# A transformer layer's expert stage, run one batch at a time, with its tokens gathered by 32-row float32 matmuls

## The reference, cut to what matters

```python
x = layernorm(h)                                   # 2 x 1024 x 128
grouped = x.reshape(B, S // 16, 16, D)             # 64 groups of 16 tokens in a batch
logits = einsum('bgtd,des->bgtes', grouped, controller) + tie     # 64 experts (es)
perm = (logits == max(logits, over the 16 tokens))                # one token for each expert and group
inner = relu(einsum('bgtesf,bgtes->bgesf', einsum('bgtd,desf->bgtesf', grouped, f1), perm))   # f = 32
inter2 = einsum('bgesf,esfd->bgesd', inner, f2)
h = h + einsum('bgesd,bgtes->bgtd', inter2, perm)
```

## Time and profile before

| what | value |
|---|---|
| median of 3 runs | 509.86 us (508.5 to 510.01) |
| the profiled execution, its own time | 509.83 us |
| its span, first to last instruction | 508.1 us |
| TensorE clock granted, mean | 0.992 of full |
| busy: PE, DVE, ACT, POOL | 485.5, 405.3, 369.7, 238.3 us |

### The profile page before, as it was taken

One profiled execution on the slowest core, in us unless ns is written; L12 is line 12 of the kernel. 1 busy time (PEld: TensorE's weight loads), 2 busy tenths in 40 slices (PEclk: granted clock), 3 DMA queues, 4 the chain that ended last, 5 costly groups with the idle time before them and its releaser, 6 DMA issues.

```text
span 508.1 us, 10652 instructions
## 1 busy us (share of the span) xinstructions
PE 485.5 (96%) x3584; PEld 396.5 (78%) x3584; DVE 405.3 (80%) x752; ACT 369.7 (73%) x696; POOL 238.3 (47%) x234
## 2 busy tenths in 40 slices
PE   2999999999999999999999999999999999998887
PEld 2955788888888888888888888888888888894564
DVE  5369999878887886788877887788778899988752
ACT  1258788887788778877888788878887887743555
POOL 1102585766356635653266536654664436443000
PEclk9999999999999999999999999999999999997999
DMA  6500029333933493361640783087308730000002
GB/s 238 200 1 0 2 53 213 79 84 78 196 67 83 83 196 65 94 124 43 141 110 10 167 167 84 11 180 153 83 10 182 151 84 0 1 2 1 1 18 68
DMA packets 29608, 44.73 MB, mean 88 GB/s; under 512 B 3328, under 2 KB 21248, under 8 KB 29312
## 3 DMA queue, kind: packets, MB, share of 16 engines
q1 hardware_dynamic: 28992, 44.21, 37.4%
q10 hardware_dynamic: 576, 0.00, 0.1%
HBM read 6.46 MB, written 1.05 MB: 15 GB/s over the span
## 4 chain that ended last, share of the span: by engine, by line
PE 89%; DVE 6%; ACT 2%; DMA 2%; issue 1%; SPq 0%; POOL 0%; DVEq 0%; ACTq 0%
PE ps L688 23%; PE ps L672 21%; PE ps L656 11%; PE ps L657 11%; PE ps L598 5%; PE ps L731 3%; PE ps L593 2%; PE ps L866 2%; PE ps L660 2%; DMA arena<-in_wqkv_rows 2%; PE ps L877 1%; PE ps L568 1%; PE ps L802 1%; DVE pt_lo L1292 1%; DVE neg_max L1304 1%; DVE v_all L1369 1%
## 5 line engine op out<-in xcount | busy, mean ns | idle before, releaser
L425 POOL TENSOR_SCALAR probs<-probs,inv_sum 128x1024 f32<-128x1024 f32 x128 | 144.7, 1131 | 183.3 <-DVE inv_sum L1298 180.6
L1304 DVE TENSOR_REDUCE neg_max<-ps 128x1 f32<-128x1024 f32 x128 | 156.7, 1224 | 63.8 <-PE ps L660 63.7
L980 ACT ACTIVATE pt_hi<-ps 128x512 fp32r<-128x512 f32 x256 | 139.1, 595 | 39.6 <-PE ps L672 39.6
L1292 DVE TENSOR_TENSOR pt_lo<-ps,pt_hi 128x512 fp32r<-128x512 f32 x256 | 162.5, 677 | 1.5 <-ACT pt_hi L980 1.5
L688 PE MATMUL ps<-pt_hi,v_slot 128*128 128x256 f32 x512 | 149.9, 326 | 0.0
L1000 ACT ACTIVATE probs<-ps,neg_max 128x1024 f32<-128x1024 f32 x128 | 142.5, 1113 | 1.5 <-DVE neg_max L1304 0.7
L672 PE MATMUL ps<-ident,probs 128*128 128x128 f32 x1024 | 133.8, 274 | 0.7 <-DVE v_all L1201 0.6
L688 PE MATMUL ps<-pt_lo,v_slot 128*128 128x256 f32 x512 | 127.4, 280 | 0.0
L672 PEld LDWEIGHTS ps<-ident,probs 128*128 128x128 f32 x1024 | 109.9, 140 | 1.3 <-DVE v_all L1201 0.7
L688 PEld LDWEIGHTS ps<-pt_hi,v_slot 128*128 128x128 f32 x512 | 96.5, 188 | 9.7 <-issue 9.7
L688 PEld LDWEIGHTS ps<-pt_lo,v_slot 128*128 128x128 f32 x512 | 97.0, 190 | 8.8 <-issue 8.8
(11 more groups left out here) (149 smaller groups left out, 434.5 us busy)
## 6 DMA issues: line engine op xcount, KB each, us to landing
q_st<-arena SPq DMA_DIRECT2D x28, 256.0 KB, 3.7
k_hi<-arena SPq DMA_DIRECT2D x28, 256.0 KB, 5.1
k_lo<-arena SPq DMA_DIRECT2D x28, 256.0 KB, 5.3
v_slot<-v_all SPq DMA_DIRECT2D x14, 512.0 KB, 3.9
arena<-arena SPq DMA_DIRECT2D x28, 256.0 KB, 5.7
f_sb<-in_f SPq DMA_DIRECT2D x2, 1024.0 KB, 10.6
x<-in_tok SPq DMA_DIRECT2D x2, 512.0 KB, 7.5
w_slot<-in_w_pairs SPq DMA_DIRECT2D x8, 128.0 KB, 2.0
```

The costliest lines, as they stand in the source:

```text
L425: pool.tensor_scalar(probs[:, t % 4, :], probs[:, t % 4, :], inv_sum[:, t % 4:t % 4 + 1], 1.0, ALU.mult, ALU.mult).then_inc(norm_done, 1)
L980: act.activation(dst, ps[:, transposes_bank(t, a, drain), :].rearrange("p (j c) -> p j c", c=P), ACT.Copy).then_inc(hi_done, 1)
L1292: dve.tensor_tensor(pt_lo[at], ps[:, transposes_bank(t, a, drain), :].rearrange("p (j c) -> p j c", c=P), pt_hi[at].bitcast(F32), ALU.subt ...
L1304: dve.tensor_reduce(neg_max[:, t % 4:t % 4 + 1], ps[:, SCORES + 2 * (t % 2):SCORES + 2 * (t % 2) + 2, :].rearrange("p a c -> p (a c)"), AX ...
```

## The change

What it does, engine by engine:

- Gathering without `quad`, `spread`, and the split into high and low parts. ScalarE (and for part of the second batch VectorE) copies the transposed choices plainly into `chosen`. Each pair of groups (32 tokens) is then gathered by one float32 matmul whose stationary operand is 32 rows of `x2` and whose moving operand is 32 rows of `chosen`, four pairs at a time on four row strips, each in its own bank (`take(b, r)`: four tiles, 16 float32 matmuls, four banks). The four results are copied, one bank at a time (`take_copy`).
- GpSimd loses `token_high` and `token_low` and two small setup instructions.
- The layer is done for one batch, then the other, with 64 groups as moving columns instead of 128: `first_product(b)` is 64 matmuls of 64 columns, in two halves of eight `k`; `second_product(b, half)` is 32 matmuls of 64 columns. Each is called twice as often as before. The first batch's gathering stands around the second's transposes; its two products around the second's choices.
- `hidden` is rectified by ScalarE in three of the four halves and by VectorE in the last.
- Rows: `row_transposes(n)` and `results(n)` handle two tiles at a time (8 transposes, 8 float32 matmuls); ScalarE copies the first bank and VectorE the second; VectorE adds 256 columns at once; SyncE stores 128 KB at a time, 8 times instead of 16.
- `LAST_OUTPUTS` is reordered: head 0 columns 0, head 1 columns 0, last values, head 0 columns 1, head 1 columns 1. VectorE makes the first batch's choices before it adds any of these, instead of after the third.

```diff
-        LAST_OUTPUTS = [(0, 0, WORK), (0, 1, TRANS), (1, 0, TRANS + 1), (1, 1, WORK)]
+        LAST_OUTPUTS = [(0, 0, WORK), (1, 0, TRANS), (0, 1, TRANS + 1), (1, 1, WORK)]
...
-                        if (k, t) == (1, 4) and pair.i == 7:
-                            pool.wait_ge(scores_ready, B * SPB - SPH)
-                            token_high(0)
-                        if (k, t) == (1, 5) and pair.i == 7:
-                            token_high(1)
...
             clear_choices(0)
-            token_low(0)
-            token_low(1)
             deviations(4)
             deviations(5)
             pool.wait_ge(logit_mm, 1)
             clear_choices(1)
-            token_low(2)
-            token_low(3)
```

TensorE's new helpers and its new list:

```diff
+            def take(b, r):
+
+                pe.wait_ge(chosen_done, 2 * b + 2)
+                if b == 1 and r == 0:
+                    pe.wait_ge(hid_left, 2)
+                for t in range(4 * r, 4 * r + 4):
+                    for j in range(PPT):
+                        if t == 4 and r == 1:
+                            take_copied(b, 0, j)
+                        rows = slice(32 * j, 32 * (j + 1))
+                        ins = pe.matmul(ps[:, TAKE_BANKS[b] + j, t % 4 * P:(t % 4 + 1) * P], x2[rows, NT * b + t, :],
+                                        chosen[rows, t, :], start=True, stop=True, tile_position=(32 * j, 0))
+                        if t % 4 == 3:
+                            ins.then_inc(taken_mm, 1)
+
+            def first_product(b):
+
+                for j in range(PPT):
+                    take_copied(b, 1, j)
+                for k in range(NK):
+                    for q in range(4):
+                        e = NK * q + k
+                        ins = pe.matmul(ps[32 * q:32 * (q + 1), HIDDEN_BANKS + k // 8, k % 8 * PAIRS:(k % 8 + 1) * PAIRS],
+                                        f1_sb[:, e * F:(e + 1) * F], taken[b][:, e, :], start=True, stop=True,
+                                        tile_position=(0, 32 * q))
...
+            def second_product(b, half):
...
+                for k in range(8 * half, 8 * half + 8):
+                    for q in range(4):
+                        rows = slice(F * q, F * (q + 1))
+                        ins = pe.matmul(ps[:, INTER_BANKS[b] + q, k % 8 * PAIRS:(k % 8 + 1) * PAIRS], f2_sb[rows, k, :],
+                                        hidden[b][rows, k, :], start=True, stop=True, tile_position=(F * q, 0))
...
             choice_transposes(0)
+            take(0, 0)
             for t in range(NT):
                 pe.wait_ge(x2_done, NT + t + 1)
                 ins = pe.transpose(ps[:, TRANS + t // 4, (t % 4) * P:(t % 4 + 1) * P], x2[:, NT + t, :], ident[:, :])
-            take(range(0, 1))
+            take(0, 1)
             pe.wait_ge(x2t_done, 4)
             expert_logits(1, PV_BANK).then_inc(logit_mm, 1)
-            take(range(1, 5))
+            first_product(0)
+            second_product(0, 0)
             choice_transposes(1)
...
+            take(1, 0)
+            second_product(0, 1)
+            take(1, 1)
+            row_transposes(0)
+            first_product(1)
+            results(0)
+            row_transposes(1)
+            second_product(1, 0)
+            results(1)
+            row_transposes(2)
+            second_product(1, 1)
+            results(2)
+            row_transposes(3)
+            for n in range(3, 8):
+                if n < 7:
+                    row_transposes(n + 1)
+                results(n)
```

ScalarE's new list, on which several steps rest:

```diff
+            choice_copy(0, 0)
+            choice_copy(0, 1)
+            for j in range(PPT):
+                take_copy(0, 0, j)
             for c in range(2):
                 act.wait_ge(x2t_mm, c + 1)
                 act.activation(x2t[:, (2 + c) * HALF:(3 + c) * HALF], ps[:, TRANS + c, :], ACT.Copy
                                ).then_inc(x2t_done, 1)
...
+            for j in range(PPT):
+                take_copy(0, 1, j)
+            rectify(0, 0)
+            rectify(0, 1)
+            inter_copies(0, 0)
+            choice_copy(1, 0)
+            take_copy(1, 0, 0)
+            take_copy(1, 0, 1)
+            inter_copies(0, 1)
+            take_copy(1, 1, 0)
+            take_copy(1, 1, 1)
+            row_copy(0)
+            rectify(1, 0)
+            row_copy(1)
+            inter_copies(1, 0)
+            row_copy(2)
+            inter_copies(1, 1)
+            for n in range(3, 8):
+                row_copy(n)
```

More of the change, by code:

```diff
@@ L541, in _ @@
             run_pairs(sp, pair_loads)
-            for t in range(TILES):
-                sp.wait_ge(result_done, t + 1)
-                sp.dma_start(out[t * P:(t + 1) * P, :], result[:, t, :]).then_inc(stored, 16)
-            sp.wait_ge(stored, 16 * TILES)
+            for n in range(TILES // 2):
+                sp.wait_ge(result_done, n + 1)
+                sp.dma_start(out[2 * n * P:2 * (n + 1) * P, :].rearrange("(t p) d -> p t d", p=P),
+                             result[:, 2 * n:2 * n + 2, :]).then_inc(stored, 16)
+            sp.wait_ge(stored, 16 * TILES // 2)
         @block.tensor
@@ new lines, in inter_copied, with row_transposes @@
+            def inter_copied(n):
+                pe.wait_ge(int_left, 2 * n + 2)
+                pe.wait_ge(int_right, 2 * n + 2)
+            def row_transposes(n):
+                b, g = ROWS[n]
+                if g == 0:
+                    inter_copied(2 * b + 1)
+                for side in range(2):
+                    for j in range(PPT):
+                        first = 2 * (NT * j + 2 * g + side)
+                        ins = pe.transpose(ps[:, ROW_BANKS[n] + side, j * P:(j + 1) * P],
+                                           inter_t[b][:, first:first + 2, :].rearrange("p u e -> p (u e)"), ident[:, :])
+                    ins.then_inc(intp_mm, 1)
@@ new lines, in results @@
+            def results(n):
+                b, g = ROWS[n]
+                pe.wait_ge(intp_left, n + 1)
+                pe.wait_ge(intp_right, n + 1)
+                if n >= 2:
+                    pe.wait_ge(result_done, n - 1)
+                for side in range(2):
+                    t = 2 * g + side
+                    for j in range(PPT):
+                        ins = pe.matmul(ps[32 * j:32 * (j + 1), RESULT_BANK + n % 2, side * D:(side + 1) * D],
+                                        perm[:, PPT * (NT * b + t) + j, :], inter_p[b][:, t, j, :],
+                                        start=True, stop=True, tile_position=(0, 32 * j))
+                ins.then_inc(res_mm, 1)
@@ L1018, in _ @@
             run_pairs(act, pair_steps)
-            def take(tiles):
-                for i in tiles:
-                    act.wait_ge(taken_mm, i + 1)
-                    act.activation(taken[:, :, 8 * i:8 * i + 8],
-                                   ps[:, TAKEN + i % 4, :].rearrange("p (g e) -> p e g", e=ES), ACT.Copy).then_inc(taken_done, 1)
             for t in range(PV_LAG):
@@ L1370, in _, with take_copy, inter_copies @@
-            for i in range(TILES):
-                dve.wait_ge(res_mm, i + 1)
-                dve.tensor_tensor(result[:, i, :], ps[:, i % 4, 0:D], h_sb[:, i, :], ALU.add).then_inc(result_done, 1)
+            def take_copy(r, j):
+                dve.wait_ge(taken_mm, PPT * (2 + r) + j + 1)
+                dve.tensor_copy(*take_parts(1, r, j)).then_inc(taken_right, 1)
+            def inter_copies(b, half):
+                dve.wait_ge(int_mm, 2 * b + half + 1)
+                for q in range(2, 4):
+                    dve.tensor_copy(*inter_parts(b, half, q)).then_inc(int_right, 1)
@@ L1375 @@
+            inter_copies(1, 0)
+            add_residual(1)
+            row_copy(2)
+            inter_copies(1, 1)
+            add_residual(2)
+            row_copy(3)
+            for n in range(3, 8):
+                if n < 7:
+                    row_copy(n + 1)
+                add_residual(n)
 SETUP_DIAG = 4
```

250 lines of the change are left out of this document (111 added, 139 removed).

## The result

The changed kernel takes 501.94 us (median of 4 runs, 501.19 to 502.61) where the kernel before, on the same chip, takes 509.18 (507.94 to 510.01): ratio 0.9861, 95% interval 0.984 to 0.9882. Measured again later it came to 501.79 (501.56 to 502.17). Predicted were 500.4, between 498.0 and 505.0. The profiled execution took 501.19 us, 499.4 of them the span.

A forecast was written before the change was run, and what follows sets the result against it. VectorE, then low-clocked TensorE, then copies, then TensorE's last loop were taken to set the pace. TensorE's 28.5 us list led to the last addition at 495.9; plus 0.6, 2.2 and 1.73 outside the span: 500.4 us, range 498.0 to 505.0.

The forecast's parts named there:

- Unit prices: Times per TensorE operation: 56 ns for a four-strip group of the 64-column first product, 109 for second product and gathering.
- The far bound of the second product: Second product with 64 columns: 56 ns for a group of four strips at best, where 109 was taken.
- the walk: Step-by-step timing of the new instruction lists from 452.71 us, putting the last addition's end at 495.93.
- The last loop: Row transposes and results at the end: 1.60 us for each pair of tiles, TensorE the bound, half the shape changes saved.
- the likeliest case: The forecast itself, 500.4 us, with no fall of TensorE's clock in the layer; chance 0.45.
- The rival of one fall: TensorE's clock falls again once, at half speed for 6.8 us, costing 1.8 us at the end: 502.2; chance 0.20.
- the slower side: Clock stays at 1.2 GHz from 462.6 us through the whole layer, end 23.2 us later, 523.6; chance 0.03.
- Waits: TensorE's waits before third gathering, first row transposes, first product 1 and last results: 1.2, 0.7, 0.4, 0.3, together 2.6 us.
- Tail: From the last addition to the span's end: 1.93 us as before plus 0.3 for the larger store, 2.2 us.
- the sum is 28.5 us: TensorE's own list from batch 0's first product at 466.74 us to 495.26: products, transposes, gatherings, results, shape changes and waits.
- fault of the walk: An unnamed error in the step-by-step timing that costs 1 to 8 us; chance 0.07.
- The rival in which the second product gains as well: Second product also gains from 64 columns: 2.8 us faster, about 497.6; chance 0.05.

The follow-up runs named there:

- e10: The changed kernel with two unused GpSimd subtractions put beside VectorE's comparisons of the second batch: 501.95 us, ratio 0.9846.
- e3: The kernel before with only its last loop changed to two tiles a turn, copies shared by ScalarE and VectorE: 506.48 us, ratio 0.9935.
- e4: The kernel before with only its gathering changed to 32-row float32 matmuls, the layer still in one piece: 513.46 us, ratio 1.0081.
- e2: The kernel before with six constant matmuls in TensorE's wait before the second batch's transposes: 508.11 us, ratio 0.9963.
- e7: The changed kernel with the first batch's second product run whole ahead of the second batch's gatherings: 502.21 us, ratio 0.9861.
- e8: The kernel before with the 32-row float32 gathering, plus 28 constant matmuls in TensorE's waits between gatherings: 510.4 us, ratio 1.0001.
- e9: The changed kernel with 72 one-column matmuls (144 instructions) in a wait ahead of the second batch's first gathering: 500.39 us, ratio 0.9819.
- e11: The changed kernel with VectorE making two copies of the first batch's second gathering, plus 60 tiny matmuls: 499.1 us, ratio 0.9792.
- e5: The changed kernel with VectorE making two of four copies of the first batch's second gathering, and choice copies moved earlier: 501.01 us, ratio 0.9832.
- e1: The changed kernel with 128 increments of an unused semaphore ahead of all TensorE work: 513.9 us, ratio 1.0082.

## Why the prediction was right, and where it was not

Right, and by its own mechanisms:
- *Unit prices.* From first product to second 1.92 us, less 0.14 for the change of shape, over 32 groups: 56 ns, as taken. By the rule of the Trainium skill (TensorE: Matmul & The Clock Gate, Part 3) that a weight load overlaps running matmuls only when its row group differs, it would have been 81 and, with the change of shape, 2.7 us, an estimate; the trace disagrees. The far bound of the second product didn't come: 64 matmul instructions take 1.95 us, change of shape included, some 113 ns for a group. A gathering call is 1.17 us with its tail: the strips run together.
- *Order at the start.* Against the earlier trace rows the logits take 1.08 us instead of 1.98 and start 6.22 us after the choice transposes (6.26 in the walk); first product 8.39 (8.53), choice transposes of batch 1 12.26 (12.35). The second batch's choices are ready at 467.50 and taken up at 469.56: 2.06 us of slack, 2.2 predicted. e10 confirms that it is slack.
- *The last loop*: 1.60 us a turn, as worked out from the earlier trace rows, and in e3 alone the loop is 2.49 us shorter.
- *Clock*: it held, as the likeliest case had it, in all nine timed runs. The rival of one fall and the slower side didn't occur. e4 shows that the slower side had substance: bursts with waits between them held the clock at 0.50 for 10 us and cost 3 us.
- *Waits*: 0.98, 0.56, 0.13 and 0.26 us, in sum 1.93, for 2.6 in the walk. *Tail*: from the last addition's end (497.16) to the span's 499.4 it is 2.24, for 2.2.

Wrong: the step "the sum is 28.5 us". Nothing in it stands for the 1.65 us of the stall, since I priced the 64-column product by its columns and its weight loads and not by the instructions it uses up. It was the "fault of the walk" to which I gave 0.07 and no name. The profile of before had only a hint of it: instruction packets on queue q8, and a first product that used up 256 instructions in 3.6 us without a gap. What a block takes, 3.3 us and more from border to border, could not be read there. The attention ended 0.73 us earlier in the profile after than in the one before, in which the change has no part; by luck that hid nearly half of the stall in the profiled run. The span was 499.4 for 498.7: -0.73 from there, -0.18 from the drain, +1.65 stall, about -0.1 from the rest. That rest is itself a balance: the waits were 0.67 shorter than walked, and small terms that I have not traced one by one make up for most of it. The median, 501.94, is 1.5 us above the 500.4.

Two figures of the working are off without touching the forecast. The rival in which the second product gains as well is priced at 2.8 us; 64 groups at 53 ns less are 3.4. And the slope of the earlier trace rows gives 26 and 103 ns for weight loads of 32 and 128 columns, not 27 and 107.

Where the gain of 7.2 us in the medians comes from is known in part. The last loop gives 2.1 us of span in e3. The clock gives 1.3 to 1.8: e2's medians differ by 1.75, and the seven runs of the kernel before at full clock have a median of 507.8 beside 509.2 here. Some 3.3 to 3.8 us are left for the drain, the gathering, the split by batches and their order, with the stall already paid. Of these only the cover over the second batch's gatherings has a price, about 1.0 us (e7). The gathering in an otherwise unchanged layer brought nothing in e4 and e8, with the reservations above, and I did not run the split with the old gathering, so what each would give alone stays open. Also not tested is which instruction kept the clock in the changed kernel: the gathering between the transposes is the likeliest, but e4 and e8 have the same code up to the logits and a clock of 1.00 (460 to 465 us) in the one and 0.53 (463 to 466.5) in the other, so whether it falls there is open to chance.

## To carry to other kernels

Where small matmuls follow each other at 7 ns an instruction, count instructions. When a whole block of 256 is used up faster than the next arrives (here 1.8 to 2.3 us, for 3.3 to 3.9 from border to border), TensorE stands idle, in a place that depends on the position in the code and not on the data. Look for "issue" gaps on TensorE with a q8 packet about 2 us ahead of their end, and shift the border so that each block holds some slower work: the same product in e9 and e11, its blocks cut elsewhere, had no gap. A cheaper gathering whose results must be copied wants something else for TensorE to do under the copies (1.0 us in e7), and TensorE's waits that it opens can cost the clock (e4). An engine made faster next to 2 us of slack brings nothing (e10); an engine idle beside a queue of four copies does (e5), once what comes behind it isn't waiting for something else.

## What the runs showed of the hardware that I had not expected

- The stall: 16 KB of instructions take 0.9 to 1.4 us to move, TensorE goes on 2.2 to 2.7 us after the packet's start, and 3.3 to 3.9 us after it passed the border before.
- A stand-alone semaphore increment on TensorE costs about 0.15 us (128 from 3.53 to 22.95 us in e1); a bf16 matmul of one column in strips, weight load included, about 10 ns (72 in 0.70 us in e9).
- The clock can rise and fall again in one stage: in e4 0.50 at 470 to 480, 1.00 at 484 to 490 and 0.51 again from 493 to 496, where the kernel before held it.
